# Two costs of a list schedule counted anew, and every engine's order searched again

## What is computed

```python
x = x + 0.5 * ffn(layernorm(x))        # layer 1
x = x + attention(layernorm(x))        # layer 2
x = x + 0.5 * ffn(layernorm(x))        # layer 3

# ffn: a shared expert for all rows, plus the two best of 8 routed experts for each row (128 -> 256 -> 128)
shared   = (silu(x @ sg.T) * (x @ su.T)) @ sd.T
probs    = sigmoid(x @ router.T + bias);  scores, idx = top_k(probs, 2)
routed   = sum over the row's 2 experts e of score_e * ((silu(x @ gate[e]) * (x @ up[e])) @ down[e])

# attention: linear, 8 heads of 16, RoPE on q and k
num = q @ (k^T v) * scale + vsum;   den = q . ksum * scale + 512
out = ((num / den + conv5(v)) * (x @ Wg.T)) @ Wo.T
```

## Time and profile before

| | |
|---|---|
| median of 3 runs | 480.28 us |
| profiled execution, span (first to last instruction; no other time is given for it) | 501.9 us |
| busy: PE / DVE / POOL / ACT | 462.0 / 346.8 / 282.3 / 271.0 us |
| mean granted TensorE clock | 0.995 |
| moves on POOL | 256, about 1 us each |
| register loads on PE's queue | 23 |

### The profile page before, as it was taken

The page is one execution under the profiler, slowest core; times in us unless marked ns, Lnnn a source line. Parts: engine busy times, 40 slices in busy tenths (PEclk is TensorE's granted clock), DMA queues, the critical chain, the costliest instruction groups (busy, mean ns, idle before and its releaser), DMA issues.

```text
span 501.9 us, 9741 instructions
## 1 busy us (share of the span) xinstructions
PE 462.0 (92%) x2975; PEld 382.8 (76%) x2975; DVE 346.8 (69%) x1064; ACT 271.0 (54%) x612; POOL 282.3 (56%) x290
## 2 busy tenths in 40 slices
PE   8979899989899999899989998999998998999896
PEld 4868678877788787688767877877776777888776
DVE  4999993333568865868889898899876532454355
ACT  5936135555476555476546664655464555565421
POOL 4148556665567245566636655686654555666562
PEclk9999999999999999999989999999999999999999
DMA  8981233253421334321132322114342253543323
GB/s 237 370 283 39 68 107 116 80 167 113 111 73 64 101 80 116 92 68 57 54 102 56 91 75 74 43 39 123 88 128 84 78 163 105 150 113 104 86 73 106
DMA packets 74353, 53.68 MB, mean 107 GB/s; under 512 B 9664, under 2 KB 68928, under 8 KB 74304
## 3 DMA queue, kind: packets, MB, share of 16 engines
q1 hardware_dynamic: 66112, 36.26, 24.4%
q0 software_dynamic: 8192, 16.79, 11.0%
HBM read 26.87 MB, written 26.15 MB: 106 GB/s over the span
## 4 chain that ended last, share of the span: by engine, by line
PE 50%; DVE 26%; issue 10%; ACT 6%; another core or an unknown queue 5%; DMA 2%; POOL 0%; SPq 0%; DVEq 0%; ACTq 0%; POOLq 0%
PE pool L888 12%; PE pool L877 6%; PE gu L843 5%; PE gu L845 5%; PE gu L844 5%; DVE X L1242 3%; PE gu L804 2%; DVE hs L1219 2%; PE pool L826 2%; DVE hs L1223 2%; PE gu L802 2%; DVE raw L1421 2%; PE gu L803 2%; DVE stats L1253 2%
## 5 line engine op out<-in xcount | busy, mean ns | idle before, releaser
L1176 POOL DMA_INDIRECT yg<-y_sorted,places x128 | 124.2, 970 | 94.3 <-PE gu L845 42.0
L1156 POOL DMA_INDIRECT x_sorted<-xn,places x128 | 129.7, 1013 | 83.3 <-PE gu L845 30.8
L1219 DVE TENSOR_TENSOR hs<-gs,gu 128x512 f32<-128x512 f32 x92 | 60.7, 663 | 89.4 <-ACT gs L1033 64.7
L1033 ACT ACTIVATE gs<-gu 128x512 f32<-128x512 f32 x124 | 72.1, 583 | 70.8 <-PE gu L804 24.8
L888 PE MATMUL pool<-w,hT 128*128 x708 | 99.3, 283 | 11.6 <-ACT hT L1039 9.7
L888 PEld LDWEIGHTS pool<-w,hT 128*128 128x128 f32 x708 | 87.6, 191 | 26.4 <-issue 23.0
L843 PE MATMUL gu<-w,xbt_hi 128*128 x177 | 81.8, 462 | 1.8 <-DVE xbt_lo L1205 1.5
L1039 ACT ACTIVATE hT<-pool 128x512 f32<-128x512 f32 x92 | 53.3, 580 | 36.2 <-PE pool L877 24.8
L845 PE MATMUL gu<-w,xbt_hi 128*128 x177 | 70.0, 396 | 0.0
L844 PE MATMUL gu<-w,xbt_lo 128*128 x177 | 69.9, 395 | 0.0
L1014 ACT ACTIVATE ys<-pool 128x256 f32<-128x256 f32 x92 | 34.5, 376 | 62.6 <-PE pool L888 34.2
(11 more groups left out here) (132 smaller groups left out, 786.8 us busy)
## 6 DMA issues: line engine op xcount, KB each, us to landing
xb<-x_sorted SPq DMA_DIRECT2D x85, 128.0 KB
y_sorted<-ys SPq DMA_DIRECT2D x85, 128.0 KB
x_sorted<-yg SPq DMA_DIRECT2D x6, 512.0 KB, 6.3
X<-x_dram SPq DMA_DIRECT2D x8, 256.0 KB, 4.8
x_sorted<-xn,places POOLq DMA_INDIRECT x128
yg<-y_sorted,places POOLq DMA_INDIRECT x128
out_dram<-X SPq DMA_DIRECT2D x8, 256.0 KB
raw<-gate_w_dram SPq DMA_DIRECT2D x4, 256.0 KB, 4.8
```

Source lines behind the costliest of these rows:

```text
L1033: nc.scalar.activation(dst, src, ACT.Silu).then_inc(silu_done, 1)
L1156: nc.gpsimd.indirect_dma_start(x_sorted[g], bass.IndirectOffsetOnAxis(places[g][:, k, t:t + 1], 0), xn[:, b, t % T], None).then_inc(scatte ...
L1176: nc.gpsimd.indirect_dma_start(yg[slot][:, k, t], None, y_sorted[g], bass.IndirectOffsetOnAxis(places[g][:, k, at:at + 1], 0)).then_inc(ga ...
L1219: v.tensor_tensor(hs[n % HB][:].rearrange("p (j i) -> p j i", j=2)[:, 0:k], gs[n % GB][:].rearrange("p (j i) -> p j i", j=2)[:, 0:k], bank ...
```

## The change

Two numbers of the planner change, and with them the table of letters that ranks the operations, all of it new. `PACE`, the least distance of two planned moves, goes from 160 to 126, which is a move's own planned length; the planned length of a load of registers goes from 40 to 6. The instructions are the same ones; their order on PE, ACT, DVE, POOL and SP is new nearly everywhere, and so are the counts that the moves wait for.

```diff
-PACE, HOP, NEAR = 160, 14, 10
+PACE, HOP, NEAR = 126, 14, 10
...
 URGENCY = (
-    "WLFWSb^ukX}PPPnPCcJNT;RELRIJR8=6@K?didXL<:VH0&UF>CSFKJaSYsKdP]JRNN5L3reTK/]YP[UOTFBVLWXSmQM{YMeWcIMPVu]/PKNPLU"
...
+    "#8Q}R#OR+-rUy}9P6n6W$g<RP/Yol)=QJY_}txGs#Ql,SXRq}o|6}dP|}eEwqz+-#9N+zcikkP}}#}#h}#jw+/z}-QU6#x}+s[@i_eXB).0i<A"
...
         if n % LOADED == 0:
-            op(("regs", r), "PE", 40, ("table", g), ("front", ("R", r - 1), 0) if r >= 1 else None)
+            op(("regs", r), "PE", 6, ("table", g), ("front", ("R", r - 1), 0) if r >= 1 else None)
```

More of the change, by code:

```diff
@@ L57 @@
-    "Pj<Q#P@dTG^:^iLP@SDUBGf<PzPf3PHRPINBKKX3KR?+tPX-PMP$PAAVqPUGLRM(TPNJiCR7Lcb2S7=RO.4.E@F[.J3RJ}J`>.=J#V@f-}4G$G"
-    "O[QKDB(fI_).6f1DC4Cs,K+V/VQPKgiHzLW.N(]$PeA4qAD&0HQVQD)/j8QBCTP+UNPGr/K5M:GTn,nPVYS/Z[RHIMKW8QJL$JKSSUHY1cHTgj"
-    "SW<[JR1alJOO8QG;?OsL9DBONB1=]h]1UOXjYPY#HDO^bK8O7HOPMM[_CKGF")
+    "#8Q}R#OR+-rUy}9P6n6W$g<RP/Yol)=QJY_}txGs#Ql,SXRq}o|6}dP|}eEwqz+-#9N+zcikkP}}#}#h}#jw+/z}-QU6#x}+s[@i_eXB).0i<A"
+    "}}zXY<r}B}UedW8IKykw}`}p}BJ,%AxsaOtft_hhEfx/q{hM}++W/wl`6p{Tjs}#a]WA|U_;{(5]7dv4d-f7}.Uae}#mi#B{#7lP{EYJgxQ{y#"
@@ new lines @@
+    "wv){x{$71|1*v|#b9#QPH}}+P7_*:kjL0]LqIAXL681<#m+q}`_##Zni,[{x##}##KYixrk.LleMw}q8lh}^)gr1WWIoum+#$R/&?VRlN}s1`&"
+    "2<E#eb7}}1}f`qRCt}s8=%#w`(PSM|<}y5dt}V{}upWsJ#:9}(+W>#s7Y%Ku_jO{T6;n##&wg(*e3t{/gRR9zuQ;3;}WQ}Q?ZD5U}wWf?_FD#+"
+    "tb_g#v%x?#`t2;4w3D#`z7#I%T=#i<]wV=-/|C[VDrLz#(Y10S}}HzYhBK8M{gHpqF[l}NH05vZJO5/e/#c)ip/u_}|r}yoR5)};rlm}exj:;%"
+    ">=0vqF{`v`uMFR`,{<SwG?:&1qu}i}Zw$hq}u{ZizfWU5uo{v4gx[e}:T}|LfxvVOeeHJEWZ|t|Q:DNA,xP9.9z*N`$u{k},/}otj(ik^Iif##"
+    "#?_sNAf#IrMS###p,<qQlF{TRg}-Xl%zPLHg4u;wk-TUVwwfy#nDV:CY{}}-g1$E}/RKCI7f)g_psQ|ETt&#OV#c#fTl0MLA}.}XI}}o|cfZQd"
@@ new lines @@
+    "X$9}GxifBs}lzEzXMqVTzO%VQyC[u{yoiE/-(Eh(`+>n>#)3#/l#;;nd&nQ?4zn&f|{QIP)4#}.#-<{pJp/{b7%c.El:p3cBqM;k&*>Ow&z8z#"
+    "2}GB(mg*d)).}u1{%@Y&yOd+#H}^_(=#&T-PT@Uf9/p)%_?0)mF.y|o&=x-7x}O,K)xR,m<N^#>,*X*?c&y=D&t{#tr[d&q)uHC}7hk}x*o)N-"
+    "Wns#8mt(T)#a4}pZppy[SU:C8g}AePKYK3)c#G}#:.}i*^sXwtyL*yHs7oD?hN#n*nsI#W[Ffr<}#$=D@lMT{0R}>A.E[/SYn>h}B/&/#}oUO}"
+    "%RwE#>S(Zb)|,?|n([x^:y)|%Bh##*?M]jWw#kc/81E8&W,M0Sy}-|H%4my-t#B}$#v5D)h)}B}q6<L%BJy<_#SN6M#@C)y(md#9P4_t1rYl*V"
+    "CRs7LU]0@y*&#qnCs.5U`n(,#BRt2,5,Ky41W`E^0np8_Oma;]rV?U2Ap}XIk6a}#<#uL-[7F:z}NL7S]?m)lJN_l@p#>pCg7lYM}R=@?b(Uag"
@@ new lines @@
+    "#}Y0g#N}4oS;5}3<tpV#gr)f#hxnhA>DhZs@p>}}(y%yr,d)A)4V|EuE}gy5lFYZa<[jmKzHa}L}}y{C9{-eC}X)}Mze>}40]#^RzW{NXF*[6}"
+    "8X_={0bZir)}}&;V_cE=#(^)R2Gt#Nl?<*i)]8Q_5ygKwd6)y#U-.plCl*qI}y*`}sd:{}Kw8E._Ife.cG(z0Z#s{=f#UXPm,S#c{X(NDn/m)c"
+    "j#4OKMr[}?l)J%IZH=T@JAx9e0^v:_^SV(W(t,UUqdU$J,i#R3#CfGHMK03z)Z.PIaibQ}&t)^#JfxF*By+dEyNKrV<2s0(JRx}/]#P+tPJ?t:"
+    "$,:ZAq7iAhz*W$i}&%^20MxTx(_TlzXsl&z){A#hwB+#VkXn?z#N}9a,j#,H-y*RkMz42n2z+$<-[2toJqQ_#+[[7[)R)UM,w)K,soV#j>M6v)"
+    "}GsaQPx>O_m608spka,(}Q/)@zZEuvOAHB(z)$H=se(dRk&O4}U]}3XK}L)k3}*t}}eGVt{wW[}PtxWLGHGU>GlA/o01)CmGM)3:BrerjXhnz4"
@@ L60 @@
+    ":#}j6`y)K#[)$X$rWkwyN{3z4O#Ks`.8k@bzS{#}}u`:4pF:6}Ou|X{N}}OH")
 BLANK = 2 * T * D
```

## The result

The changed kernel takes **474.12 us** (median of 4 runs, 473.74 to 475.32) against 479.58 us for the kernel before on the same chip (4 runs): a ratio of 0.9883, 95% interval 0.9859 to 0.9907. Measured again (experiment 9) it was 474.21 us, ratio 0.9875 (0.9833 to 0.9918). The forecast of 476.0 us, faster, held; how it came about did not, as the experiments show.

A forecast was written before the change was run, and what follows sets the result against it. PE's stream, 92% busy with many short stalls, was taken as the bound. Terms -3.9 - 2.1 - 2 + 3.5 = -4.5 us of the 501.9 us span, times 0.957, -4.3 from 480.28: 476.0 us, range 469 to 484.

The forecast's parts named there:

- What bounds the kernel: Whole kernel: PE's stream, busy 92% of 501.9 us, with many short stalls, each at a place in the order.
- Register loads, 0: Loads of registers in PE's queue, 0.598 us each, 23 times: none removed or made shorter, so directly 0.
- what stands behind them, -3.9 us: Hidden transposes behind register loads: a front moves in between, saving 0.43 us at nine places; bounds 0 and -4.7 us.
- The sign that was named for this term: Hidden transposes would wait for `hid` clearly less often than 20 times in their weight loads.
- Rival 1: Stalls only change place, from hidden transposes to `down`: about 480 us; chance 0.27 together with Rival 3.
- Rival 3: Register loads really cost PE 0.6 us and the new order piles work behind them; chance 0.27 together with Rival 1.
- Layer 1's shared experts, -2.1 us: DVE nearly full there: `probs` (third group) and `table` (second) leave the way of shared `hid`; bounds 0 and -3 us.
- that sign: The first routed front would start about 2 us before 67.2 us.
- Attention spread out, -2: Attention of batches 2 to 7 among more routed pairs, removing batch 2's 1.67 us wait at layer 3's transpose; bounds 0, -5.
- tighter, +3.5 us: Less PE work before `den` in four batches (2.4 us of stalls) and `project` in two (1.8 us); bounds 0 and +6.
- Moves at 126, 0: Closer planned moves: last scatter to first pair transpose hardly shorter, so no gain; bounds -1 and +8 us.
- Rival 2: Moves come late at the closer spacing and pair transposes wait for loaded rows: slower, about 484 us; chance 0.18.

The follow-up runs named there:

- experiment 9: The changed kernel, unaltered, measured again: 474.21 us, ratio 0.9875 to the kernel before.
- experiment 8: Kernel before with its old order on every engine, but the planned times using the two new numbers (126 and 6): 479.77 us, ratio 0.9986.
- experiment 2: Kernel before with nine hidden transposes behind a register load and a down product swapped with the routed front after them: 480.37 us, ratio 1.0005.
- experiment 11: Kernel before with nine hidden transposes moved behind the next front, and eight of their down products behind the following pair transpose: 478.09 us, ratio 0.9965.
- experiment 6: Old order for the plan's first 60 us on every engine, new order for all the rest: 476.02 us, ratio 0.9917 to the kernel before.
- experiment 1: The kernel before, unchanged, profiled a second time: measured 483.19 us, span 481.3 us.
- experiment 3: Kernel before with three DVE operations moved later: probs and best of the third group, table of the second: 482.44 us, ratio 1.0014.
- experiment 5: New order for the plan's first 60 us on every engine, old order for all the rest: 479.21 us, ratio 0.9972 to the kernel before.
- experiment 12: Changed kernel with ten stalling PE operations each placed behind the next front half: 477.03 us, ratio 0.9972 to the kernel before.
- experiment 7: Kernel before with batch 2's shared down product, and its addition on DVE, placed later in the start: 481.03 us, ratio 1.0018.

## Why the prediction was right, and where it was not

The number was near because terms too large on both sides, and one never seen, made up for each other: that is luck in the number. PE's stalls after 75 us by kind, in us, and the rest of the execution:

| | old order (8) | transposes later (2) | with `down`s (11) | old start, new rest (6) | changed (9) |
|---|---|---|---|---|---|
| hidden transposes | 7.1 | 3.9 | 4.3 | 4.4 | 4.8 |
| `down` | 4.8 | 7.2 | 4.9 | 5.7 | 6.0 |
| pair transposes | 2.7 | 3.3 | 3.2 | 1.0 | 1.9 |
| attention's five products | 0.6 | 0.5 | 0.6 | 2.1 | 2.1 |
| rest, from the first pair transposes | 406.5 | 406.4 | 405.0 | 402.9 | 405.2 |

- **What bounds the kernel.** Right: the same products, fewer stalls between them. The times per place were read from an execution that was not typical, above all the waits of `down`.
- **Register loads, 0, and what stands behind them, -3.9 us.** The place was right, the size not. The step that failed is the choice of the inner value over the bound that stood beside it, "0, if the wait only moves to `down`, which still stands about 1.04 us behind": with the transposes alone that bound is what came (experiment 2), with the same 1.04 us. A pair goes through two distances, 1.57 us from fronts to transposes and 1.37 from transposes to `down`, and a stall goes only when both are covered. The new order covers both, with a pair transpose more in between; in the old order the same edit gave 0.35% or 1.7 us by the medians and 0.6 to 1.5 at like clock (experiment 11), of the 2.60 us there were. The sign that was named for this term failed: the weight loads of the hidden transposes wait for `hid` 23 times, 9.0 us, after the change, and 23 times, 9.6 us, in experiment 1; the waits became shorter, not fewer. Rival 1 was thus right for the edit that the prediction described, and wrong for the one that the new order makes.
- **Rival 3, and "directly 0".** The loads do cost PE something in the old order, of which the sum had nothing. Where a load is long and PE has little issued ahead of it, PE runs dry until its end. In experiment 1 the load of R40 takes 1.31 us, to 214.71, and the pair transposes behind it start 0.06 us later, after 0.71 us of idling:

```profile
214.76 0.41 PE L826 MATMUL pool<-squares_sb,xb 128*128 128x128 f32 x2 [0.71 <-issue]
```
```profile
L814 PEldq TENSOR_LOAD <-offsets x1: 1307/1307/1307, 213.4 to 213.4; - x1
```

  Three pair transposes, each right behind a load, wait so, 1.9 us in all (`issue` in the list of experiment 1), and 1.9 to 2.1 us in the six other traces with the old order behind the start; in the first profile of before it is 0.9 us, also in three. None does in the changed kernel or with the old start and the new rest. There the load of R40 takes 1.31 us as well, but attention products stand ahead of the transposes and run meanwhile. So rival 3 had a cost right, and its outcome wrong: the new order covers these loads. No run tried this by itself.
- **Layer 1's shared experts, -2.1 us.** The three operations that the term named are worth nothing by themselves (experiment 3). The new start as a whole gives 0.28% or 1.3 us in front of the old rest (experiment 5), and nothing there at like clock. In the changed kernel it does come sooner: its first pair transposes start at 62.39 us against 64.13 in the first profile of before, both with the clock at 1.00, and the wait of 1.38 us in front of the last shared unit is 0.18. The first routed front came 2.3 us before 67.2, as foretold, but that sign was not of the named cause:

```profile
62.39 0.38 PE L826 MATMUL pool<-squares_sb,xb 128*128 128x128 f32 x2
...
64.88 0.48 PE L843 MATMUL gu<-w,xbt_hi 128*128 x1
```

- **Attention spread out, -2, and tighter, +3.5 us.** The wait of 1.67 us has no counterpart in the second profile of before, whose longest wait of that line is 0.6 us (experiment 1) and whose clock is 1.00 in both windows of the earlier trace rows: there was less to win than 2 us. All waits of that line together are 1.6 us there and 0.7 after the change. The tighter distances cost less than was counted, and not where it was counted. None of the four `den`s waits. Batch 2's starts 1.70 us after its `kv`, as soon as the 0.78 us of work between the two is issued (194.75 to 195.53), where 1.5 us were counted:

```profile
193.83 1.16 PE L955 MATMUL pool<-v_tok,k_rot 128*128 128x130 f32 x8
194.75 0.48 PE L843 MATMUL gu<-w,xbt_hi 128*128 x1
...
195.53 1.04 PE L964 MATMUL pool<-ks_bd,raw 128*128 128x8 f32 x8
```

  Of the two `project`s batch 4's waits 0.46 us and batch 1's not at all. The 0.3 us of `den` in the waits above is batch 6's, `project` of batch 3 waits 0.47, and all stalls of attention's products rose from 0.6 to 2.1 us: +1.5 in place of +3.5, most of it at places that the term did not name. These two were not tried alone.
- **Moves at 126, 0.** Right, to 0.36% (experiment 8). POOL's timeline of the changed kernel shows the close spacing, here 1.27 us, that was counted on:

```profile
40.50 0.96 POOL L1156 DMA_INDIRECT x_sorted<-xn,places  x1 [0.30 <-issue]
41.77 0.97 POOL L1156 DMA_INDIRECT x_sorted<-xn,places  x1 [0.30 <-issue]
```

  Rival 2 (moves come late) did not happen: PE waits for loaded rows 1.4 us in all, 2.1 in the second profile of before. The window of these moves has DVE busy 19.04 of 20 us, as full as before:

```profile
40.00:60.00 20.00, 19.07 (x130) 16.16 (x130) 19.04 (x57) 8.84 (x20) 13.82 (x14) 1.00 0.13 48
```

  The Trainium skill (SBUF — State Buffer, section "SBUF: two separate sides") has a DVE operation with two SBUF inputs lock out a GpSimd operation that reads SBUF. The trace agrees. The 16 scatters from 36.48 to 58 us take 1.04 us on average, with DVE as full as it is, but two of them take 1.44 and 1.40 us; both begin while DVE runs line 1455, whose operands `raw` and `w` both lie in SBUF:

```profile
52.14 1.44 POOL L1156 DMA_INDIRECT x_sorted<-xn,places  x1 [0.35 <-PE gu L804]
...
56.70 1.40 POOL L1156 DMA_INDIRECT x_sorted<-xn,places  x1 [0.30 <-issue]
```
```profile
52.06 0.69 DVE L1455 TENSOR_TENSOR w<-raw,w 128x512 fp32r<-128x512 f32 x1
...
56.57 1.89 DVE L1455 TENSOR_TENSOR w<-raw,w 128x512 fp32r<-128x512 f32 x3
```

  Of the 256 moves in this trace 12 take 1.20 to 1.57 us, and each of the 12 begins while DVE runs an operation of over 0.5 us on two tensors that both lie in SBUF; 227 begin at other times, and the longest of those takes 1.17 us. So it is what DVE reads, and not how busy it is, that goes with a long move. How much of PE's 1.4 us of waits for loaded rows comes of it was not tested.
- **What the sum had not.** The pair transposes' stalls fell by 0.8 to 1.7 us, for the most part at the loads above. And the clock: in the runs beside experiments 1, 5, 9 and 12 the kernel before has medians of 480.6, 480.4, 479.7 and 478.8 us, and 478.7, 478.3, 477.4 and 477.7 in those at a mean clock of 0.998 and above. The changed kernel keeps the full level, so 1.1 to 2.3 us of its gain over the median of before is clock. That this clock is lost in the start shows in seven of the profiles (experiments 1, 2, 3, 5, 7, 8 and 11); why the changed kernel keeps it, and the same start with the old rest does not, stays open.

Put together: about 2 us of clock; some 1.4 to 1.7 us in the start (experiment 6 against the changed kernel at full clock, 475.6 and 474.2 us; 64.13 and 62.39 us to the first pair transposes); and behind it 0.8 to 2.9 us, as the rest of the changed kernel takes 405.2 and 405.3 us in its two profiles and the old rest 406.0 to 408.0 in five with the clock at 1.00 there (experiments 1, 2, 5, 7 and 8); experiment 6 against the kernel before gives 2.7. The runs give 5.5 to 6 us. In the rest the nine places make 1.7 us by their stalls and the pair transposes behind loads about 1.9 by their idle time; attention's products take 1.5 back, and what else the new order wins and loses there is not parted. The split between clock and stalls is read from the clock of each run and from the profiles, and was not tested by a change of its own.

## What to carry to other kernels

In a strict order an operation that waits is a symptom: before it is moved, add up what the whole chain behind it needs from stage to stage, and move it only if every distance is covered after the move, since otherwise the same stall stands at the next stage or becomes longer. Tables of ranks belong to the costs they were searched with; a cost is tested by keeping the order and changing the times, not by ranking anew. And a profile whose span is far from the median of the runs is first taken again, before any place in it is given a price.

## What was not expected of the hardware

The same program, profiled twice, had spans of 501.9 and 481.3 us, and the difference was no lower clock (0.995 and 0.989): waits of ACT and DVE without a releaser, 19.5 us in one group alone, were spread over the routed part of one and absent from the other. What they were no run here tells.

In the old start PE idles for 3.0 us at 28 to 31 us, and in many executions the granted clock then falls from 2.4 to 1.2 GHz for a while; in some it does not, though the wait is there (the first profile of before and experiment 6's have it, 3.0 us, and the clock stays at 1.00 through the start). The stretch from 30 to 40 us in experiment 1 and in the first profile of the same kernel, with the clock behind the five busy times:

```profile
30.00:40.00 10.00, 8.86 (x35) 8.20 (x36) 6.28 (x28) 3.01 (x7) 3.96 (x4) 0.51 0.52 147
```
```profile
30.00:40.00 10.00, 8.58 (x57) 7.50 (x58) 9.30 (x39) 6.08 (x13) 6.22 (x6) 1.00 0.52 157
```

35 products against 57 in the same 10 us of the same kernel, and 3.4 us later at the first pair transposes (67.53 against 64.13): an idle stretch of 3 us can cost more behind it than in it.
